# Second attention of a gated transformer block: the inversion of the sums on ACT moved between two fours of exponentials, the division moved on VectorE

## The chip, the cores and the metric

The kernel runs on one core of a Trainium2 chip. The metric is the device time of one execution in microseconds (us). The engines are TensorE (PE, with its weight loads as PEld), VectorE (DVE), ScalarE (ACT), GpSimd (POOL) and SyncE (SP). Each runs its own instructions in program order, and they wait for each other on semaphores.

## The reference

Four stages follow one another on x of 32 batches x 128 rows x 128 columns: an attention over a context, six layers of local attention with an MLP, a second attention over the same context, and a quantised matrix product. The change lies in the third. Cut to what matters there:

```python
x = x + tanh(g_xattn[1]) * L1_xattn(layernorm(x), ctx, ctx)       # the third stage
x = x + tanh(g_ffn[1]) * L1_ffn(layernorm(x))                      # the fourth

# L1_xattn, 16 heads of 8 columns, for each batch
scores = einsum('bhqd,bhkd->bhqk', Qh, Kh) / sqrt(8)
scores = scores - max(scores, axis=-1)
attn = softmax(scores, axis=-1)
attn = clip(attn, 1e-12, None)
attn = attn / sum(attn, axis=-1)          # the second division: the sums inverted on ACT
ctx = einsum('bhqk,bhkd->bhqd', attn, Vh)
return ctx @ Wo.T + bo
```

## The kernel before

The stages run one after another. The last two are one pipeline, written in `second_attention`: a loop over steps from -18 to 47, in which each engine issues a fixed list of calls, each for a batch that lies some steps ahead or behind. `@each(NB)` drops the calls whose batch does not exist, and `@opening` keeps one in four, those that begin a group of four batches (128 rows each, so 512 columns). So the work of four successive steps repeats. In this text a **0-step** is a step whose number is a multiple of four, and the 1-step, 2-step and 3-step follow it.

What a batch b goes through, by the functions' names:

- PE `scores(b, half)` (L1337) makes the scores of heads 0 to 7 and 8 to 15, each half into two banks of PSUM of its own. It waits until the exponentials of batch b-1 have read that half (`exped[half]`).
- DVE `row_maxima(b, half)` (L1589) takes the maxima of the half, one step early for half 0.
- ACT `exponentials(b, half)` (L1480) makes eight exponentials of 128x128, one a head, each with its sum. It signals `exped[half]` after the eighth.
- DVE `invert(b, half)` (L1596) inverts these first sums, and POOL `normalise(b, half)` (L1710) multiplies by them.
- PE `transpose_weights(b, t)` (L1347) turns four heads, t = 0 to 3, called t0 to t3 below: t0 and t1 one step later, t2 and t3 two steps later. DVE `clip_weights(b, t)` (L1604) clips each into `probsT`.
- PE `mix(b)` (L1361 and L1365), in step b+2, multiplies the clipped weights by v and by ones. The second product is the sum that the clipped weights are divided by. It waits for the clipped t3 (`clipped`).
- ACT `invert_sums(b)`, in step b+2, inverts that sum as exp(-ln): one ACTIVATE with Ln (L1489) and one with Exp (L1491), both 128x128. It waits for `mixed`, and signals `den_inverted`.
- DVE `divide_mix(b)` (L1613), in step b+2, multiplies the mixed values by it and signals `mix_made`.

Four banks of PSUM rotate among all other products of PE (`ROTATING`). `Banks.fill` makes PE wait until the last user of a bank has been read. A bank that `mix` filled is free when `divide_mix` has signalled. By the table of turns, the next user of the bank of a 3-step's mix is t3 in the 0-step that follows; of a 0-step's mix it is `transpose_x`, of a 1-step's `project_out`, of a 2-step's t3 in the 3-step. The bank that `project_k` fills in a 1-step goes to t3 of the 2-step. It is free when DVE and ACT `bias_k` (L1581, L1452) have made the keys.

What else occurs once in four steps and is named below: in a 0-step ACT `copy_x` (L1509); in a 1-step PE `transpose_x` (L1383) and `project_k` (L1309), ACT `copy_steps` (L1528) and `bias_k`, DVE `row_stats` (L1623, L1627) and `bias_k`; in a 2-step ACT `square` (L1435) and `place_v` (L1472), DVE `rescale` (L1669) and `row_amax` (L1636); in a 3-step ACT `bias_q` (L1461) and `root` (L1441, L1443), DVE `row_scale` (L1643) and `quantise` (L1653, L1656, L1660). The functions on rows belong to the fourth stage and begin some steps later than the attention.

The lists of PE's calls in a step, which the change leaves alone (each opening one stands in its own kind of step only):

```python
scores(step, 0); transpose_weights(step - 2, 2); project_out(step - 6); mean(step + 6)
transpose_weights(step - 2, 3); transpose_x(step - 9); scores(step, 1); multiply(step - 14)
transpose_weights(step - 1, 0); transpose_steps(step - 13); project_q(step + 1)
mix(step - 2); transpose_weights(step - 1, 1); project_k(step + 3); variance(step + 5); project_v(step + 2)
```

Of the kernel before, what the change touches and what calls it, by code (L numbers as in the profile page):

```python
# [64 lines left out]
def each(n):  # L65

    def of(stage):
        def run(u, *more):
            if 0 <= u < n:
                stage(u, *more)  # L70
        return run
    return of
# [46 lines left out]
def build(nc, dram):  # L119
    stack = ExitStack()  # L120
    with stack:
# [3 lines left out]
        def sem(name):  # L125
            return stack.enter_context(nc.semaphore(name))
# [1058 lines left out]
        def second_attention(phase):  # L1185
# [43 lines left out]
            scored, maxed, exped, normalised = ([sem(f"x1_{k}{half}") for half in range(2)] for k in ("scored", "maxed", "exped", "normalised"))  # L1229
# [33 lines left out]
            def bank(stage, n):  # L1263
                return psum[:, bank_of[stage, n], :]
# [159 lines left out]
            def act(act):  # L1424
# [4 lines left out]
                @each(NB)  # L1429
                @opening  # L1430
                def square(g):
                    act.wait_ge(ln_centred_made, before + g + 1)
                    if g >= 2:
                        act.wait_ge(ln_scaled, before + g - 1)
                    act.activation(spread[g % 2][:, :], centred[g % 2][:, :], ACT.Square).then_inc(ln_squared, 1)  # L1435
# [19 lines left out]
                @each(NB)  # L1455
                @opening
                def bias_q(g):
                    act.wait_ge(q_projected, g + 1)
                    if g >= 2:
                        act.wait_ge(scored[1], GB * (g - 1))  # L1460
                    act.activation(queries[g % 2][:, :], bank("q", g), ACT.Identity, bias=b_q, scale=inv_root).then_inc(biased_act, 1)  # L1461
# [10 lines left out]
                    act.copy(places[:, :, :, 0:XD], bank("v", g).rearrange("p (m j d) -> p j m d", j=4, d=XD)).then_inc(v_placed, 1)  # L1472

                @each(NB)
                def exponentials(b, half):
                    act.wait_ge(maxed[half], b + 1)
                    if b >= 2:
                        act.wait_ge(turned, TURNS * (b - 2) + 2 * half + 2)
                    for h in range(8 * half, 8 * half + 8):
                        e = act.activation(expo[b % 2][:, h, :], psum[:, 4 + h // 4, (h % 4) * S:(h % 4 + 1) * S], ACT.Exp,  # L1480
                                           bias=negmax[b % 2][:, h:h + 1], accum_out=total[b % 2][:, h:h + 1])
                    e.then_inc(exped[half], 1)

                @each(NB)
                def invert_sums(b):
                    act.wait_ge(mixed, b + 1)
                    if b >= 2:
                        act.wait_ge(mix_made, b - 1)
                    act.activation(rden[b % 2][:, :], bank("mix", b)[:, S:2 * S], ACT.Ln).then_inc(den_logged, 1)  # L1489
                    act.wait_ge(den_logged, b + 1)  # L1490
                    act.activation(rden[b % 2][:, :], rden[b % 2][:, :], ACT.Exp, scale=-1.0).then_inc(den_inverted, 1)  # L1491
# [30 lines left out]
                @each(NB)  # L1522
                @opening
                def copy_steps(g):
                    act.wait_ge(steps_turned, g + 1)
                    if g >= 2:
                        act.wait_ge(multiplied, g - 1)
                    act.copy(stepsT[g % 2][:, :], bank("tq", g)[:, 0:GT // 2].bitcast(BF16)).then_inc(steps_copied, 1)  # L1528

                for step in range(FIRST, LAST):  # L1530
                    exponentials(step, 0)
                    square(step + 6)
                    copy_steps(step - 13)
                    bias_q(step + 1)
                    invert_sums(step - 2)
                    exponentials(step, 1)
                    place_v(step + 2)
                    row_root(step - 9)
                    bias_k(step + 3, 2)
                    bias_k(step + 3, 3)  # L1540
                    root(step + 5)
                    copy_x(step - 8)
                    gate_out(step - 5)

            def dve(dve):
# [29 lines left out]
                @each(NB)  # L1575
                @opening
                def bias_k(g, j):
                    dve.wait_ge(k_projected, g + 1)
                    if g >= 2:
                        dve.wait_ge(scored[1], GB * (g - 1))  # L1580
                    dve.tensor_scalar(keys[g % 2][:, j, :], bank("k", g), head_parts[:, j:j + 1], b_k_part[:, j:j + 1],  # L1581
                                      ALU.mult, ALU.add).then_inc(biased_dve, 1)

                @each(NB)
                def row_maxima(b, half):
                    dve.wait_ge(scored[half], b + 1)
                    if b >= 2:
                        dve.wait_ge(exped[half], b - 1)
                    dve.tensor_reduce(negmax[b % 2][:, 8 * half:8 * half + 8], pairs[2 + half].rearrange("p (h n) -> p h n", h=8),  # L1589
                                      axis=X, op=ALU.max, negate=True).then_inc(maxed[half], 1)  # L1590

                @each(NB)
                def invert(b, half):
                    t8 = total[b % 2][:, 8 * half:8 * half + 8]
                    dve.wait_ge(exped[half], b + 1)
                    dve.reciprocal(t8, t8).then_inc(inverted, 1)  # L1596
# [10 lines left out]
                @each(NB)  # L1607
                def divide_mix(b):
                    g = b // GB
                    dve.wait_ge(den_inverted, b + 1)  # L1610
                    if g >= 2:
                        dve.wait_ge(out_made, g - 1)
                    dve.tensor_tensor(mixedT[g % 2][:, (b % GB) * S:(b % GB + 1) * S], bank("mix", b)[:, 0:S], rden[b % 2][:, :],  # L1613
                                      ALU.mult).then_inc(mix_made, 1)
# [57 lines left out]
                for step in range(FIRST, LAST):  # L1672
                    clip_weights(step - 2, 2)
                    centre(step + 6)
                    clip_weights(step - 2, 3)
                    row_scale(step - 11)
                    rescale(step - 14)
                    row_maxima(step, 1)
                    clip_weights(step - 1, 0)
                    if step > FIRST:  # L1680
                        residual(step - FIRST)
                    invert(step, 0)
                    row_amax(step - 10)
                    quantise(step - 11)
                    row_stats(step - 9)
                    divide_mix(step - 2)
                    clip_weights(step - 1, 1)
                    bias_k(step + 3, 0)
                    row_maxima(step + 1, 0)
                    invert(step, 1)  # L1690
                    bias_k(step + 3, 1)
# [208 lines left out]
```

## Time and profile before

| what | us |
|---|---|
| median of 3 runs | 3399.71 |
| lowest and highest | 3399.1, 3406.09 |
| the profiled execution, its own time | 3404.29 |
| its span, first to last instruction | 3402.5 |
| of that the last two stages, from about 3060 to the end | 342.5 |
| of that the steps 0 to 31 with their drain, from the first scores at 3096 | 306 |

The profiled execution took 1.8 us more than its span, and lies 4.6 us above the median of the runs. Busy times of the whole span (PE 95%, DVE 86%, ACT 70%, POOL 78%) are those of the six layers before; they say nothing of the last 340 us. A group of steps is read there from four views: the windows (busy time of each engine and the granted TensorE clock), the timeline of one engine with the idle time before each row, one line's instructions with what they wait for, and the chain of waits. All times in the rows are microseconds from the span's start.

### The profile page before, as it was taken

Reading aid. Unit: us, or ns where it says so; the run is one execution under the profiler, and the core shown is the slowest. Engines: PE = TensorE matmul, PEld = TensorE weight load, DVE = VectorE, ACT = ScalarE, POOL = GpSimd, SP = SyncE. Lnnn points to the kernel's source line nnn. Section 1 sums busy time; section 2 is a strip of 40 time slices with the busy share of each in tenths; the row PEclk is TensorE's granted clock in tenths of the full one; section 3 lists DMA queues with packets and bytes.
Section 4 is the critical chain, followed back from the end, with each engine's and each line's share of the span. In section 5 each row is a group of like instructions: output and inputs, shape, how many; then the busy total and the mean of one; then the engine's idle time right before and its main releaser. Section 6 shows DMA issues by size and latency. Waiting matters only on the chain. (4 is left out here: it accounts for less than half of the span.)

```text
span 3402.5 us, 130907 instructions
## 1 busy us (share of the span) xinstructions
PE 3247.4 (95%) x56355; PEld 2059.5 (61%) x56386; DVE 2942.0 (86%) x3343; ACT 2379.8 (70%) x4288; POOL 2640.0 (78%) x1408
## 2 busy tenths in 40 slices
PE   8977999999999999999999999999999999977996
PEld 4544666666666666666666666666666666643554
DVE  6869999999999999999989899998999999935887
ACT  6865676767676667777677776776767676746895
POOL 1218988888888888888888888888888888833576
PEclk9989999999999999999999999999999999988998
DMA  2001433333433343333433334343344333340000
GB/s 94 2 1 56 121 114 114 121 121 115 119 112 114 120 126 120 114 114 122 126 111 117 114 111 129 117 120 114 114 126 126 118 111 113 109 125 1 2 11 17
DMA packets 229189, 336.06 MB, mean 99 GB/s; under 512 B 39046, under 2 KB 151044, under 8 KB 228228
## 3 DMA queue, kind: packets, MB, share of 16 engines
q1 hardware_dynamic: 228612, 327.68, 31.5%
q8 instruction: 446, 7.31, 0.9%
q14 instruction: 131, 1.07, 0.1%
HBM read 124.14 MB, written 102.76 MB: 67 GB/s over the span
## 5 line engine op out<-in xcount | busy, mean ns | idle before, releaser
L733 PE MATMUL psum<-w_qkv,f_xs 128*128 128x512 f32 x2304 | 1078.3, 604 | 12.3 <-DVE f_times_sin L1027 7.6
L1154 POOL TENSOR_TENSOR f_rotated<-f_times_cos,f_times_sin 128x1024 f32<-128x1024 f32 x384 | 908.4, 2366 | 8.8 <-DVE f_times_sin L1027 8.8
L1162 POOL TENSOR_TENSOR f_rotated<-f_rotated,f_rnorm 128x1024 f32<-128x1024 f32 x384 | 723.0, 1903 | 31.8 <-ACT f_rnorm L908 4.9
L733 PEld LDWEIGHTS psum<-w_qkv,f_xs 128*128 128x128 f32 x2304 | 409.8, 191 | 395.1 <-issue 375.2
L897 ACT ACTIVATE f_squares<-psum 128x1024 f32<-128x1024 f32 x384 | 393.0, 1023 | 341.0 <-PE psum L733 335.9
L1146 POOL TENSOR_TENSOR f_probs<-f_probs,f_rowsum 128x1024 f32<-128x1024 f32 x192 | 365.4, 1903 | 322.3 <-DVE f_rowsum L1066 322.3
L1026 DVE TENSOR_TENSOR f_times_cos<-psum,rot 128x1024 f32<-128x1024 f32 x384 | 470.0, 1224 | 121.8 <-ACT f_squares L897 117.7
L915 ACT COPY f_qkT<-psum 128x1024 f32<-128x1024 f32 x384 | 369.9, 1013 | 210.2 <-PE psum L743 210.2
L1027 DVE TENSOR_TENSOR f_times_sin<-psum,rot 128x1024 f32<-128x1024 f32 x384 | 466.4, 1214 | 0.0
L1034 DVE TENSOR_REDUCE f_sumsq<-f_squares 128x16 f32<-128x1024 f32 x384 | 463.8, 1210 | 0.0
L743 PEld LDWEIGHTS psum<-consts,f_rotated 128*128 128x128 f32 x3072 | 348.6, 141 | 96.3 <-issue 87.6
L743 PE MATMUL psum<-consts,f_rotated 128*128 128x128 f32 x3072 | 371.2, 274 | 16.2 <-POOL f_rotated L1162 13.3
L1140 POOL TENSOR_TENSOR f_probs<-f_probs,f_negmax 128x1024 f32<-128x1024 f32 x192 | 365.0, 1901 | 0.0
L787 PEld LDWEIGHTS psum<-f_probsT,f_v 64*64 64x64 f32 x6144 | 262.7, 135 | 162.5 <-issue 162.5
L801 PE MATMUL psum<-f_outT,w_o 128*128 128x256 f32 x1536 | 358.9, 387 | 1.2 <-ACT f_outT L929 1.2
L760 PEld LDWEIGHTS psum<-f_qkT 64*32 64x32 f32 x24576 | 254.0, 105 | 146.9 <-issue 143.1
L787 PE MATMUL psum<-f_probsT,f_v 64*64 64x64 f32 (+1 forms) x6144 | 309.7, 228 | 15.6 <-issue 15.6
L801 PEld LDWEIGHTS psum<-f_outT,w_o 128*128 128x128 f32 x1536 | 285.8, 191 | 45.2 <-issue 1.8
L787 PE MATMUL psum<-f_probsT,f_v_moved 64*64 64x32 f32 (+1 forms) x12288 | 307.1, 217 | 0.0
L760 PE MATMUL psum<-f_qkT 64*32 64x64 f32 x24576 | 285.2, 226 | 1.3 <-issue 1.3
L787 PEld LDWEIGHTS psum<-f_probsT,f_v_moved 64*64 64x64 f32 x12288 | 285.8, 136 | 0.0
L828 PE MATMUL psum<-f_xn,w 128*128 128x512 f32 (+1 forms) x576 | 278.3, 607 | 7.4 <-ACT f_xn L971 7.4
(175 smaller groups left out, 5173.5 us busy)
## 6 DMA issues: line engine op xcount, KB each, us to landing
f_v_moved<-f_v SPq DMA_DIRECT2D x768, 128.0 KB, 2.8
turned_blocks<-w_qkv SPq DMA_DIRECT2D x192, 512.0 KB, 3.0
f_probsT<-turned_blocks SPq DMA_DIRECT2D x768, 128.0 KB, 2.8
w_qkv<-in_l_wqkv SPq DMA_DIRECT2D x18, 512.0 KB, 4.2
w_o<-in_l_wo SPq DMA_DIRECT2D x6, 512.0 KB, 4.5
w_qkv<-in_ctxT SPq DMA_DIRECT2D x1, 2048.0 KB, 8.7
out<-x_f_result SPq DMA_DIRECT2D x8, 256.0 KB, 2.2
w<-in_l_w SPq DMA_DIRECT2D x6, 341.0 KB
```

Source lines behind the costliest of these rows:

```text
L733: mm = pe.matmul(pairs[i][:, j * BANK:(j + 1) * BANK], xs[g % 2][:, u % GB, :], w_qkv[:, part * INNER + j * BANK:part * INNER + (j + 1) * ...
L743: tr = pe.transpose(pairs[i][:, t * S:(t + 1) * S], rotated[u % 2][:, part, 2 * t:2 * t + 2, :].rearrange("p h d -> p (h d)"), ident)
L760: mm = pe.matmul(pairs[i][these, at:at + NEAR], qkT[u % 2][rows, 0, t, these], qkT[u % 2][rows, 1, t, near], start=True, stop=True, tile_p ...
L787: mm = pe.matmul(pairs[i][cols, at + windows.start * WIN:at + windows.stop * WIN], values, probsT[u % 2][rows, windows, j, :], start=True, ...
L801: mm = pe.matmul(pairs[i][:, 0:GT // 2], w_o[:, t, :], outT[:, t, tokens], start=t == 0, stop=t == IT - 1)
L897: act.activation(squares[part][:, :], pair("qk"[part], u), ACT.Square).then_inc(squared[part], 1)
L915: act.copy(qkT[u % 2][:, part].rearrange("p t n -> p (t n)"), pair(("qT", "kT")[part], u)).then_inc(copied[part], 1)
L1026: dve.tensor_tensor(halves(times_cos[part][:, :]), halves(taken), table(0), ALU.mult)
L1027: dve.tensor_tensor(halves(times_sin[part][:, :]), halves(taken)[:, ::-1], table(1), ALU.mult).then_inc(producted[part], 1)
L1034: dve.tensor_reduce(sumsq[u % 2][:, part * H:(part + 1) * H], squares[part][:, :].rearrange("p (s h d) -> p h s d", s=2, h=H), axis=XY, op ...
L1154: pool.tensor_tensor(rotated[u % 2][:, part].rearrange("p h (s d) -> p s h d", s=2), halves(times_cos[part][:, :]), halves(times_sin[part] ...
L1162: pool.tensor_tensor(rt, rt, rnorm[u % 2][:, part * H:(part + 1) * H].unsqueeze(2).broadcast_to([P, H, HD]), ALU.mult).then_inc(normalised ...
```

## The change

ACT's exponentials of a half can now be issued in part, by the first and the last head. Half 0 is issued whole. Half 1 is issued as two fours, and the inversion of the sums, which stood ahead of half 1, now stands between them. `exped[1]` is signalled behind the second four, as before behind the eighth. On DVE the division moves two places back: behind `clip_weights(step - 1, 1)` and the first `bias_k`, ahead of `row_maxima(step + 1, 0)`. Nothing is added, removed or resized, and PE and POOL keep their order.

```diff
@@ -1472,14 +1472,15 @@
                 @each(NB)
-                def exponentials(b, half):
+                def exponentials(b, half, first, last):
                     act.wait_ge(maxed[half], b + 1)
                     if b >= 2:
                         act.wait_ge(turned, TURNS * (b - 2) + 2 * half + 2)
-                    for h in range(8 * half, 8 * half + 8):
+                    for h in range(8 * half + first, 8 * half + last):
                         e = act.activation(expo[b % 2][:, h, :], psum[:, 4 + h // 4, (h % 4) * S:(h % 4 + 1) * S], ACT.Exp,
                                            bias=negmax[b % 2][:, h:h + 1], accum_out=total[b % 2][:, h:h + 1])
-                    e.then_inc(exped[half], 1)
+                    if last == 8:
+                        e.then_inc(exped[half], 1)
@@ -1528,12 +1529,13 @@
                 for step in range(FIRST, LAST):
-                    exponentials(step, 0)
+                    exponentials(step, 0, 0, 8)
                     square(step + 6)
                     copy_steps(step - 13)
                     bias_q(step + 1)
+                    exponentials(step, 1, 0, 4)
                     invert_sums(step - 2)
-                    exponentials(step, 1)
+                    exponentials(step, 1, 4, 8)
                     place_v(step + 2)
@@ -1683,9 +1685,9 @@
                     row_stats(step - 9)
-                    divide_mix(step - 2)
                     clip_weights(step - 1, 1)
                     bias_k(step + 3, 0)
+                    divide_mix(step - 2)
                     row_maxima(step + 1, 0)
```

ACT in a 3-step and the beginning of the 0-step behind it, before (L1461 is `bias_q`, L1441 and L1443 `root`; the names behind waits are semaphores):

```order
L1461 ACTIVATE x_queries<-psum,x_vecs 128x512 [waits x1_scored1,x1_q_projected]
L1489 ACTIVATE x_rden<-psum 128x128 [waits x1_mix_made,x1_mixed]
L1491 ACTIVATE x_rden<-x_rden 128x128 [waits x1_den_logged]
L1480 ACTIVATE x_expo,x_total<-psum,x_negmax 128x128 [waits x1_turned,x1_maxed1]
L1480 ACTIVATE x_expo,x_total<-psum,x_negmax 128x128 x7
L1441 ACTIVATE x_spread<-psum,eps 128x512 [waits ln_variance_made]
L1443 ACTIVATE x_spread<-x_spread 128x512 [waits ln_logged]
```

The same place after:

```order
L1461 ACTIVATE x_queries<-psum,x_vecs 128x512 [waits x1_scored1,x1_q_projected]
L1480 ACTIVATE x_expo,x_total<-psum,x_negmax 128x128 [waits x1_turned,x1_maxed1]
L1480 ACTIVATE x_expo,x_total<-psum,x_negmax 128x128 x3
L1490 ACTIVATE x_rden<-psum 128x128 [waits x1_mix_made,x1_mixed]
L1492 ACTIVATE x_rden<-x_rden 128x128 [waits x1_den_logged]
L1480 ACTIVATE x_expo,x_total<-psum,x_negmax 128x128 [waits x1_turned,x1_maxed1]
L1480 ACTIVATE x_expo,x_total<-psum,x_negmax 128x128 x3
L1441 ACTIVATE x_spread<-psum,eps 128x512 [waits ln_variance_made]
L1443 ACTIVATE x_spread<-x_spread 128x512 [waits ln_logged]
```

Four exponentials moved ahead of the two ACTIVATEs of the inversion; it is the same in every other step, whatever stands around.

DVE from the end of `quantise` in a 3-step into the 0-step behind it, before:

```order
L1660 TENSOR_SCALAR x_f_steps<-x_f_cen 128x512 [waits f1_quantised]
L1613 TENSOR_TENSOR x_mixedT<-psum,x_rden 128x128 [waits x1_out_made,x1_den_inverted]
L1604 TENSOR_SCALAR x_probsT<-psum 128x512 [waits x1_mixed,x1_turned]
L1589 TENSOR_REDUCE x_negmax<-psum 128x8 [waits x1_exped0,x1_scored0]
L1596 RECIPROCAL x_total<-x_total 128x8 [waits x1_exped1]
L1604 TENSOR_SCALAR x_probsT<-psum 128x512 [waits x1_mixed,x1_turned] x2
```

The same place after (lines of DVE stand two higher in the changed file):

```order
L1662 TENSOR_SCALAR x_f_steps<-x_f_cen 128x512 [waits f1_quantised]
L1606 TENSOR_SCALAR x_probsT<-psum 128x512 [waits x1_mixed,x1_turned]
L1615 TENSOR_TENSOR x_mixedT<-psum,x_rden 128x128 [waits x1_out_made,x1_den_inverted]
L1591 TENSOR_REDUCE x_negmax<-psum 128x8 [waits x1_exped0,x1_scored0]
L1598 RECIPROCAL x_total<-x_total 128x8 [waits x1_exped1]
L1606 TENSOR_SCALAR x_probsT<-psum 128x512 [waits x1_mixed,x1_turned] x2
```

The division and the clip of t1 changed places.

DVE in a 1-step, from the end of `row_stats`, before:

```order
L1627 BN_AGGR x_f_meanvar<-x_f_stats 128x2 x3
L1613 TENSOR_TENSOR x_mixedT<-psum,x_rden 128x128 [waits x1_out_made,x1_den_inverted]
L1604 TENSOR_SCALAR x_probsT<-psum 128x512 [waits x1_mixed,x1_turned]
L1581 TENSOR_SCALAR x_keys<-psum,consts,x_bk_part 128x512 [waits x1_scored1,x1_k_projected]
L1589 TENSOR_REDUCE x_negmax<-psum 128x8 [waits x1_exped0,x1_scored0]
```

The same place after:

```order
L1629 BN_AGGR x_f_meanvar<-x_f_stats 128x2 x3
L1606 TENSOR_SCALAR x_probsT<-psum 128x512 [waits x1_mixed,x1_turned]
L1583 TENSOR_SCALAR x_keys<-psum,consts,x_bk_part 128x512 [waits x1_scored1,x1_k_projected]
L1615 TENSOR_TENSOR x_mixedT<-psum,x_rden 128x128 [waits x1_out_made,x1_den_inverted]
L1591 TENSOR_REDUCE x_negmax<-psum 128x8 [waits x1_exped0,x1_scored0]
```

Here the division also passed the first part of the keys.

## Rows read from the trace of the kernel before

**Rows 1.** Windows over four steps: us, busy (x) of PE PEld DVE ACT POOL, clock.

```profile
3273.80:3308.30 34.50, 31.45 (x384) 19.24 (x384) 29.65 (x58) 31.06 (x149) 24.18 (x17) 1.00 0.03 9
```

**Rows 2.** Line L1489, the Ln of the inversion: its instructions and their waits.

```profile
L1489 ACT ACTIVATE x_rden<-psum x32: 277/277/334, 3117.6 to 3375.5; 128x128 f32<-128x128 f32 x32
  PE psum L1365: 22.1, 27
```

**Rows 3.** ACT's waits from 3130 to 3330: us in total, times, longest.

```profile
ACT x_rden L1489 <- PE psum L1365: 12.1, 21, 2.0
```

**Rows 4.** Timeline of ACT, a 0-step: start, us, row, [idle before <-releaser].

```profile
3267.01 0.37 ACT L1480 ACTIVATE x_expo<-psum,x_negmax 128x128 f32<-128x128 f32 x1 [0.61 <-DVE x_negmax L1589]
...
3269.42 0.40 ACT L1480 ACTIVATE x_expo<-psum,x_negmax 128x128 f32<-128x128 f32 x1
...
3270.35 0.28 ACT L1489 ACTIVATE x_rden<-psum 128x128 f32<-128x128 f32 x1 [0.44 <-PE psum L1365]
...
3270.88 0.35 ACT L1480 ACTIVATE x_expo<-psum,x_negmax 128x128 f32<-128x128 f32 x1
```

**Rows 5.** Timeline of ACT, a 2-step in which the inversion did not wait.

```profile
3321.13 0.42 ACT L1480 ACTIVATE x_expo<-psum,x_negmax 128x128 f32<-128x128 f32 x1
3321.47 0.33 ACT L1489 ACTIVATE x_rden<-psum 128x128 f32<-128x128 f32 x1
...
3322.06 0.35 ACT L1480 ACTIVATE x_expo<-psum,x_negmax 128x128 f32<-128x128 f32 x1
```

**Rows 6.** Timeline of PE, the same 0-step (t3, t0, mix) into the 1-step.

```profile
3265.30 0.66 PE L1347 MATMUL psum<-consts,x_expo 128*128 128x128 f32 x4 [0.52 <-DVE x_mixedT L1613]
...
3266.95 0.66 PE L1347 MATMUL psum<-consts,x_expo 128*128 128x128 f32 x4
3268.34 1.08 PE L1361 MATMUL psum<-x_probsT,x_vpad 128*32 128x128 f32 x32 [0.74 <-issue]
...
3273.81 1.13 PE L1337 MATMUL psum<-x_keys,x_queries 32*128 32x512 f32 x4 [0.41 <-ACT x_expo L1480]
```

**Rows 7.** Timeline of DVE, from the 3-step through the 0-step.

```profile
3264.96 0.28 DVE L1613 TENSOR_TENSOR x_mixedT<-psum,x_rden 128x128 f32<-128x128 f32 x1
3265.16 0.68 DVE L1604 TENSOR_SCALAR x_probsT<-psum 128x512 f32<-128x512 f32 x1
3265.76 1.21 DVE L1589 TENSOR_REDUCE x_negmax<-psum 128x8 f32<-128x1024 f32 x1
...
3267.00 1.24 DVE L1604 TENSOR_SCALAR x_probsT<-psum 128x512 f32<-128x512 f32 x2
...
3271.00 0.29 DVE L1613 TENSOR_TENSOR x_mixedT<-psum,x_rden 128x128 f32<-128x128 f32 x1 [0.86 <-ACT x_rden L1491]
```

**Rows 8.** Timeline of DVE, `row_maxima` of half 0 in a 1-step.

```profile
3245.72 1.23 DVE L1589 TENSOR_REDUCE x_negmax<-psum 128x8 f32<-128x1024 f32 x1 [0.23 <-PE psum L1337]
```

**Rows 9.** Timelines of ACT and PE in the first groups, before `quantise` has begun.

```profile
3125.66 0.28 ACT L1489 ACTIVATE x_rden<-psum 128x128 f32<-128x128 f32 x1 [0.72 <-PE psum L1365]
...
3136.44 1.13 PE L1337 MATMUL psum<-x_keys,x_queries 32*128 32x512 f32 x4 [1.06 <-ACT x_expo L1480]
...
3169.22 1.13 PE L1337 MATMUL psum<-x_keys,x_queries 32*128 32x512 f32 x4 [0.62 <-ACT x_expo L1480]
```

**Rows 10.** Chain of waits, from the 1-step into the 2-step: start, us, what.

```profile
3247.98 1.39 issue
```

**Rows 11.** The drain: ACT in a 1-step, and PE's t3 after the last batch's scores.

```profile
3345.24 0.28 ACT L1489 ACTIVATE x_rden<-psum 128x128 f32<-128x128 f32 x1 [0.19 <-PE psum L1365]
...
3364.61 0.66 PE L1347 MATMUL psum<-consts,x_expo 128*128 128x128 f32 x4 [3.02 <-DVE x_mixedT L1613]
```

**Rows 12.** The clock: PE's window (us, busy, clock), ACT in that 2-step, ACT in a later one.

```profile
3180.70:3183.90 3.20, 3.20 (x52) 0.55 0.02 5
...
3184.86 0.28 ACT L1489 ACTIVATE x_rden<-psum 128x128 f32<-128x128 f32 x1 [1.97 <-PE psum L1365]
...
3253.77 0.28 ACT L1489 ACTIVATE x_rden<-psum 128x128 f32<-128x128 f32 x1 [0.53 <-PE psum L1365]
```

## The prediction, made before the changed kernel was run

> **What bounds the kernel now.** The change touches only the last two stages, some 300 of 3400 us, so I read those. First the windows over four steps: in their middle they repeat to 0.1 us, 34.5 us each (three groups, of which one row stands for all), with PE busy 31.4, ACT 31.1 and DVE 29.6 of them at a clock of 1.00 [rows 1]. No engine is full, and three are nearly so; the time is then set by a loop of waits that passes through all three, and a wait that goes is worth only what the next one allows.
>
> Next the line of the inversion: 27 of its 32 Ln wait for the mix's second product, 22.1 us in all [rows 2], 12.1 of them in the 200 us between 3130 and 3330 [rows 3]. That is what the change can remove. Last the timelines and the chain, to see in which steps that wait lies on the loop. I follow a group from scores of half 1 in a 1-step to the same place four steps later:
>
> - From the 1-step to the 2-step the loop runs through PE's scores, the maxima on DVE, the keys on DVE and then on ACT. PE's t3 of the 2-step wants the bank of `project_k` and stands 1.39 us, which the chain calls issue [rows 10], since it names no releaser; by the table of banks it is ACT's keys. ACT's own speed does not matter in this piece, as it waits for DVE's keys itself.
> - From there to the 3-step PE runs without a gap, and from its scores for the 3-step DVE runs without one through `quantise` and into the 0-step. ACT's waits of the 2-step (0.53 [rows 12]) and of the 3-step (0.73, the same pattern) are not on the loop: at its end ACT stands 0.61 us for DVE's maxima in any case [rows 4].
> - In the 0-step DVE clips t2 and t3 until 3268.24 [rows 7], the mix starts at 3268.34 [rows 6], and ACT, done with half 0, stands 0.44 us for the mix before it can invert [rows 4]. Then come the eight exponentials of half 1, and PE stands 0.41 us for them [rows 6]. This wait is on the loop, once in four steps.
>
> **The change part by part.**
>
> *The wait of a 0-step.* With an exponential last started at 3269.42 and the next free place 0.34 later, ACT would begin half 1 at 3269.76. It began at 3270.88 [rows 4], 1.12 later, of which an inversion that waits for nothing takes 0.59 (3321.47 to 3322.06 [rows 5]). So 0.53 us is removed from ACT there: the mix ends at 3270.3, four exponentials at 0.34 end at 3271.1, and the inversion then finds its sum ready. The eighth exponential ends 0.53 earlier. PE can use only 0.41 of it, since that is how long it stood [rows 6]; then its own work, which began with the mix, is last. **0.41 us a group.** It holds for the five groups between 3169 and 3341, which have the same gap of 0.41: 5 x 0.41 = 2.05 us.
>
> *The two groups before them* have no `quantise`, DVE is not last, and ACT's wait in the 3-step (0.72 [rows 9]) counts: ACT gains 0.72 + 0.06 = 0.78, and PE stood 1.06 at the end of the first and 0.62 at the end of the second [rows 9]. The first gives 0.78, the second 0.62: 1.40 us. In the steps ahead of them the inversion waited for nothing, or not yet ran: nothing.
>
> *The drain.* In the last group no keys are made, so that the waits of the 0-step and the 1-step (0.53, and 0.19 + 0.06 [rows 11]) add up on ACT, and POOL's normalisation hands on 0.78 where PE took 0.41 of it: 0.37 us more.
>
> *The division moved on DVE.* It now stands behind one clip, 0.60 from start to start [rows 7], and in a 1-step also behind the first keys. Where DVE was waiting for ACT it fills the wait: in the 0-step DVE stood 0.86 us [rows 7], and the clip of t1 fits in. The inverted sum now comes at about 3271.7 in place of 3270.97, the division ends near 3272.0, just when `row_maxima` can start. In the 3-step DVE has no gap, the sum of its work is the same, and only the order changes: `row_maxima` starts as before, and the division is 0.60 later. PE's t3 of the 0-step waits for just that: 0.52 us before [rows 6], about 1.1 now. Behind t3 are queued the scores of half 1, t0 and the mix. They would be done 0.60 later, but the mix waits for the clipped t3 anyway, and that gap is 0.74 [rows 6]. So 0.14 us of cover is left, and I cost it at nothing. Without the cover each of six groups would lose up to 0.19: 0.60 less the 0.41 that PE has to spare. In the 1-step `row_maxima` stood 0.23 for PE's scores [rows 8]; the keys now start when `project_k` ends and the division (0.21 from start to start) ends 0.1 us ahead of the scores. Nothing, with little to spare. In the drain t3 is waited for with no cover: the clip of t3 comes 0.15 later than it would. I take 0.15 off.
>
> *The split itself.* One more instruction with waits a step, which are met. Where one half follows another with its wait, the start comes 0.34 to 0.36 behind the last, so at most 0.02 x 32 = 0.6 us of ACT, on the loop in a quarter of the steps: 0 to 0.2, taken as 0.1.
>
> **The sum:** 2.05 + 1.40 + 0.37 - 0.15 - 0.1 = 3.6 us less. The profiled execution would go from 3404.3 to 3400.7, its span from 3402.5 to 3398.9. The median of the runs is 4.6 us below the profiled one; by it 3399.7 - 3.6 = **3396.1 us**. That is 0.11% less. About 0.2%, or 6.8 us, is what a measurement of this kernel can tell from no change, so I forecast a gain that is hardly seen.
>
> **Rivals.**
>
> *All of ACT's wait counts.* ACT is busy 31 of 34.5 us [rows 1], and if my loop is wrong and ACT sets it, every removed microsecond shows: 12.1 us in 200, over the 237 us from the first inversion to 3355, is 14.3 us, giving 3385.4. Half of it, 7 us, is the point from which it is a measurable gain. For it speaks that PE waits for ACT's exponentials in most 0-steps. Against it stand PE's gap of 0.41 as a cap, and the 0.61 us in which ACT waits for DVE with no regard to the inversion [rows 4, 6].
>
> *PE is last everywhere.* If PE's 0.41 is in truth covered (a weight load or the bank behind it), the exponentials gain nothing that PE can take, and only the first groups stay: 3398 to 3400, no change.
>
> *The later division starves PE, and its clock falls.* This is the one that ends slower. Its place is t3 of the 0-step, where PE's wait goes from 0.52 to 1.1 us. The clock did fall to the 1.2 GHz level once in these stages, to a mean of 0.55 from 3180.7 to 3183.9 [rows 12]; PE had just had the gap of 1.38 ahead of t3 in that 2-step. ACT then waited 1.97 for the mix where it waits 0.53 in the same place of later groups [rows 12], so a fall costs 1.44. If the longer wait brought one in each of the six groups from the first `quantise` on, and the cover of 0.14 failed too, the cost is 6 x (1.44 + 0.19) = 9.8 us: 3409.5. It decides from about two falls on, where 2 x 1.63 = 3.3 has eaten most of the gain. Against it: the other gaps of 1.39 us in later groups brought no fall, the clock of whole groups stays at 1.00 [rows 1], and PE's idle time as a whole shrinks by the 0.41.
>
> The Trainium skill ("TensorE: Matmul & The Clock Gate", section "HAM oscillation — how this bites in real kernels") says that PE's short idles between groups of matmuls can make the clock go up and down, and this speaks against lengthening a wait of PE. By it the time would be that of this rival, 3409.5; by the rows, in which such gaps recur without a fall, it is that of the sum. I go by the rows.
>
> **How the numbers follow.** My forecast, 3391 to 3400: 0.62. PE last everywhere, 3398 to 3401: 0.17. ACT's wait counting half or whole, 3385 to 3393: 0.14. Starved PE, 3401 to 3410: 0.07. Faster by over 0.2% (below 3392.9) comes from the third and an edge of the first: 0.16. Slower by over 0.2% (above 3406.5) is half of the last and a bit of spread, as one of three runs lay at 3406.09: 0.05. Within 0.2%: 0.79. The range from 3390 to 3401.5 leaves out the lower part of the third and most of the last.
>
> **What would show it.** Right: the line of Ln has almost no idle time before it outside the drain; the period goes from 34.5 to about 34.05 us; PE's gap ahead of scores of half 1 in 1-steps is gone, and its gap ahead of t3 in 0-steps is about 1.1 us; ACT's wait for the maxima in 0-steps and for the keys in 1-steps is larger than before (0.61 for the maxima), since ACT arrives earlier at both. Wrong: a period below 33.8 (then ACT was last in more steps than one); a period of 34.4 or more, with the mix of the 0-step starting later after the clip of t3 than 0.1 us, or DVE's maxima in the 1-step behind the division and not behind the scores; or a clock under 1.00 in more than one group. A single fall of the clock that comes or goes moves the result by 1.4 us and would say nothing of the change.

## The result, and the profile after

| kernel | median of 8 runs, us | lowest and highest |
|---|---|---|
| before | 3404.2 | 3397.32, 3408.96 |
| changed | 3416.41 | 3410.62, 3420.55 |

The ratio is 1.0029, 95% interval 1.0015 to 1.0043. So the changed kernel is slower by 0.3%, about 10 us (5 to 15), where the prediction said 3.6 us faster. The time lies above its range. Some 4.5 us of the distance to the predicted 3396.1 are not the change's: the median of the kernel before is 3404.2 with eight runs, where the prediction had three runs and 3399.71. A second round of runs later gave 1.0013 (0.9998 to 1.0028), on the same side, but by itself not told from no change.

The stages ahead of the second attention vary by some microseconds from one execution to the next: the first scores of half 0 began at 3096.32 in the profile before and at 3103.10 in the one after. What the change does is read better from there to the end of the span. I call it **the stage** below: 3402.5 - 3096.3 = 306.2 us before, 3418.2 - 3103.1 = 315.1 us after. It grew by 8.9 us.

The windows over four steps of the changed kernel (us, busy (x) of PE PEld DVE ACT POOL, then the granted clock as a share of 2.4 GHz), for [rows 1]:

```profile
3214.50:3249.80 35.30, 32.77 (x385) 20.39 (x384) 29.60 (x58) 31.16 (x148) 24.17 (x17) 0.95 0.03 9
3249.80:3286.80 37.00, 34.47 (x385) 20.99 (x384) 29.69 (x58) 31.26 (x148) 24.19 (x18) 0.91 0.03 9
```

A group of steps takes 35.3 to 37.0 us in place of 34.5. DVE's and ACT's busy times are as before (29.6 and 31.1 to 31.3). PE is busy for 1.4 to 3.1 us more with the same instructions, and the clock is below 1.00. The timeline of PE in the 0-step of the second window, for [rows 6] (start, us, row, idle before):

```profile
3276.31 0.79 PE L1347 MATMUL psum<-consts,x_expo 128*128 128x128 f32 x4 [1.15 <-DVE x_mixedT L1615]
3277.04 2.07 PE L1337 MATMUL psum<-x_keys,x_queries 32*128 32x512 f32 x4
3279.04 1.11 PE L1347 MATMUL psum<-consts,x_expo 128*128 128x128 f32 x4
3280.09 1.94 PE L1361 MATMUL psum<-x_probsT,x_vpad 128*32 128x128 f32 x32
3281.80 1.90 PE L1365 MATMUL psum<-x_probsT,x_ones 128*32 128x128 f32 x32
```

t3 waits 1.15 us for the division, where it waited 0.52. Behind it scores take 2.07 in place of 1.13 and the mix 1.94 in place of 1.08. The clock of these few microseconds is that of the lower level, 1.2 GHz:

```profile
3276.30:3283.60 7.30, 7.29 (x76) 0.53 0.12 36
3265.50:3276.30 10.80, 9.67 (x101) 1.00 0.01 2
```

(PE's window: us, busy, clock.) Ahead of the wait the clock was at 2.4 GHz. The Trainium skill ("TensorE: Matmul & The Clock Gate", section "A second HAM failure mode: psum-queue depth-cycling") tells of another kernel in which short idles of PE between groups of matmuls make the clock go up and down. In this profile the trace agrees: 0.53 of full speed behind a wait of 1.15 us.

ACT in the same 0-step, for [rows 4]:

```profile
3277.43 0.37 ACT L1480 ACTIVATE x_expo<-psum,x_negmax 128x128 f32<-128x128 f32 x1 [1.36 <-DVE x_negmax L1591]
...
3283.77 0.28 ACT L1490 ACTIVATE x_rden<-psum 128x128 f32<-128x128 f32 x1 [1.84 <-PE psum L1365]
```

Four exponentials now stand ahead of the inversion, and still it waits 1.84, because the mix is late by more than they take. Over the line as a whole (us, times) the wait has shrunk from 22.1 [rows 2] to:

```profile
  PE psum L1365: 14.5, 9
```

of which 6.17 and 1.49 are in the drain. DVE did what its new order says, for [rows 7]:

```profile
3240.05 0.68 DVE L1606 TENSOR_SCALAR x_probsT<-psum 128x512 f32<-128x512 f32 x1
3240.65 0.28 DVE L1615 TENSOR_TENSOR x_mixedT<-psum,x_rden 128x128 f32<-128x128 f32 x1
3240.85 1.22 DVE L1591 TENSOR_REDUCE x_negmax<-psum 128x8 f32<-128x1024 f32 x1
```

### The profile page after: what moved, and what is told of

Same layout as the page of the kernel before. It is cut to its first block and busy times, and to the rows that moved or that the text cites. A ratio compares the mean times of both kernels' runs of the same rounds, so it can differ in the third digit from the quotient of the medians.

```text
span 3418.2 us, 130937 instructions
## 1 busy us (share of the span) xinstructions
PE 3264.5 (96%) x56355; PEld 2067.2 (60%) x56386; DVE 2942.0 (86%) x3343; ACT 2381.3 (70%) x4288; POOL 2640.0 (77%) x1408
```

## The experiments

I count a **fall** where the first product of a mix takes 1.5 us or more in place of 1.08. (One row of `after_again` has only 4 of its 32 records; there the second product starts 1.70 us after the first, as behind the other falls.) Other falls lie in the 2-steps 6 and 10 and in the drain; they make the stage longer, and the count of four leaves them out. Four 0-steps of each profile count for the wait of t3: those of the steps 12, 16, 20 and 24, from the first `quantise` to the drain. `dve_long`, `fill_half`, `fill_one`, `shift_once` and `dve_again` were run once each, for the profile, and have no ratio. "Period" is from one such group to the next, by the transposes of x.

| kernel | edit | ratio (95%) | stage, us | t3's wait in 0-steps | falls in those four | period without, with fall |
|---|---|---|---|---|---|---|
| before | | | 306.2 | 0.52 | 0 | 34.46 |
| changed | both | 1.0029 (1.0015-1.0043) | 315.1 | 1.15 | 4 | -, 35.3 to 37.0 |
| after_again | both | 1.0013 (0.9998-1.0028) | 315.0 | 1.15 | 4 | -, 35.3 to 37.0 |
| act_only | split only | 1.0016 (1.0005-1.0027) | 311.6 | 0.55 | 0 | 35.03 |
| dve_only | later division only | 0.9993 (0.9984-1.0002) | 305.0 | 1.10 | 0 | 34.46 |
| dve_again | the same | | 304.9 | 1.10 | 0 | 34.46 |
| late_in_3 | division later in 3-steps only | 0.9992 (0.9982-1.0002) | 310.0 | 1.11 | 1 | 34.46, 37.44 |
| back_in_3 | both, division back in 3-steps | 0.9982 (0.9971-0.9992) | 301.9 | 0.55 | 0 | 33.98 |
| back_again | the same | 0.9982 (0.9969-0.9995) | 304.7 | 0.55 | 0 | 33.98 |
| fill_gap | both, 4 transposes in the wait | 0.9992 (0.9978-1.0005) | 301.2 | 0.71 | 0 | 33.98 |
| fill_half | both, 2 transposes | | 305.0 | 0.93 | 0 | 33.98 |
| fill_one | both, 1 transpose | | 304.9 | 1.04 | 0 | 33.98 |
| pad_in_1 | both, 4 transposes in 1-steps | 1.0011 (0.9997-1.0025) | 313.8 | 1.15 | 3 | 34.41, 35.8 to 37.4 |
| shift_once | both, 12 transposes once | | 301.3 | 1.15 | 0 | 33.97 |
| dve_long | division only, later still | | 320.7 | 2.24 | 3 | 35.39, 37.0 to 39.9 |
| turns | back_in_3 and other banks | 0.9992 (0.9981-1.0003) | 302.5 | 0.31 | 0 | 33.13 |
| turns2 | the same, in all steps | 0.9977 (0.9964-0.9991) | 299.5 | 0.31 | 0 | 33.13 |

The theory after the result was the rival of the prediction: the later division makes PE wait longer ahead of t3, and its clock falls. Against it stood that the split of the exponentials costs the time, or that the falls are chance.

### Each half of the change alone

`act_only` has the split with the division at its old place:

```diff
+                    exponentials(step, 1, 0, 4)
                     invert_sums(step - 2)
-                    exponentials(step, 1)
+                    exponentials(step, 1, 4, 8)
```

> The exponentials of half 1 in two fours with the inversion between them, as in the changed kernel; the division on DVE stays where it was before. If the later division makes the loss (PE's t3 of a 0-step waits 1.15 us and the clock falls behind it): that wait is 0.5 us again, the granted clock of the groups from the first quantise on is 1.00, their period 34.1 to 34.5 us, the ratio to before 0.999 to 1.000. If the split of the exponentials makes the loss: periods of 35 to 37 us and a ratio of 1.002 to 1.003, as in the changed kernel. If falls of the clock are chance: some groups with one and some without, in this as in the others.

t3's wait in the 0-step was short and there was no fall behind it, as the first expectation had it, but the period of 35.03 and the ratio of 1.0016 lie near what was expected if the split made the loss. The reason is another wait. DVE in a 1-step:

```profile
3213.80 0.29 DVE L1615 TENSOR_TENSOR x_mixedT<-psum,x_rden 128x128 f32<-128x128 f32 x1 [1.04 <-ACT x_rden L1492]
3214.01 0.68 DVE L1606 TENSOR_SCALAR x_probsT<-psum 128x512 f32<-128x512 f32 x1
3214.60 0.80 DVE L1583 TENSOR_SCALAR x_keys<-psum,consts,x_bk_part 128x512 f32<-128x512 f32 x1
```

The inverted sum comes later, by the four exponentials, and DVE stands 1.04 us for it with the clip, the keys and the maxima queued behind. The keys then reach ACT late, and PE's t3 of the 2-step waits 2.40 in place of 1.39. The period is 35.03. In one such 2-step the clock fell too:

```profile
3253.99 0.63 PE L1347 MATMUL psum<-consts,x_expo 128*128 128x128 f32 x4 [2.40 <-issue]
...
3256.86 1.94 PE L1361 MATMUL psum<-x_probsT,x_vpad 128*32 128x128 f32 x32
```

DVE stands so long in each 1-step from the first `quantise` to the drain. So the split needs the division moved in the 1-steps. It is the 3-steps in which the move hurts.

`dve_only` is the reverse, and `late_in_3` the smallest edit that lengthens the wait:

```diff
+                    if step % 4 != 3:
                         divide_mix(step - 2)
                     clip_weights(step - 1, 1)
                     bias_k(step + 3, 0)
+                    if step % 4 == 3:
+                        divide_mix(step - 2)
```

> The division on DVE stands later as in the changed kernel; ACT's order stays as before. Later division: t3 of a 0-step waits 1.1 us, clock of a group 0.91 to 0.95, period 36 to 37 us, ratio 1.002 to 1.004 (ACT's wait for the mix stays, so up to 0.001 worse than the changed kernel). Split: as before, period 34.5, ratio 1.000.

> The kernel before, but in the 3-steps alone the division stands behind the clip of t1. It is the smallest edit that lengthens PE's wait. Later division: t3 of a 0-step waits 1.1 us, the clock falls in most groups, ratio 1.002 to 1.004. Any other cause: 1.000.

Both missed. The wait was 1.10, as said, but the time did not change: in `dve_only` the clock fell in none of the four 0-steps, in `late_in_3` in one. Here are two waits of `late_in_3`, one with a fall and one without:

```profile
3226.68 0.66 PE L1347 MATMUL psum<-consts,x_expo 128*128 128x128 f32 x4 [1.12 <-DVE x_mixedT L1613]
...
3230.19 1.94 PE L1361 MATMUL psum<-x_probsT,x_vpad 128*32 128x128 f32 x32
```

```profile
3263.90 0.66 PE L1347 MATMUL psum<-consts,x_expo 128*128 128x128 f32 x4 [1.11 <-DVE x_mixedT L1613]
...
3266.34 1.08 PE L1361 MATMUL psum<-x_probsT,x_vpad 128*32 128x128 f32 x32
```

It also shows that the later division costs nothing when the clock holds: the period of `dve_only` is 34.46, as before. The cover of 0.14 us ahead of the mix was there.

### The division back in the 3-steps

`back_in_3` keeps both halves of the change and takes the division back where DVE has no gap:

```diff
+                    if step % 4 == 3:
+                        divide_mix(step - 2)
                     clip_weights(step - 1, 1)
                     bias_k(step + 3, 0)
+                    if step % 4 != 3:
                         divide_mix(step - 2)
```

> The changed kernel, but in the 3-steps alone the division stands before the clip of t1 again. Later division: t3 of a 0-step waits 0.5 us, no fall of the clock from the first quantise on, period 34.0 to 34.1, ratio 0.9985 to 0.9995, which is the gain of the sum (3.6 us). If any of the other edits costs the time, the ratio stays at 1.002 to 1.003.

> The changed kernel with the division back in the 3-steps, once more, beside the next one on the same chip. The stage from the first scores to the end was 301.4 us in its first profile against 306.2 before. Again no fall of the clock between the first quantise and the drain, period 33.98, stage 301 to 303, ratio 0.997 to 0.999.

The ratio was 0.9982 twice. The period is 33.98 with no fall in eight 0-steps of two profiles:

```profile
3253.64 0.66 PE L1347 MATMUL psum<-consts,x_expo 128*128 128x128 f32 x4 [0.55 <-DVE x_mixedT L1615]
...
3256.67 1.08 PE L1361 MATMUL psum<-x_probsT,x_vpad 128*32 128x128 f32 x32 [0.74 <-issue]
...
3261.13 0.60 PE L1383 MATMUL psum<-consts,xres 128*128 128x128 f32 x4
```

The stage took 301.9 us in the first profile and 304.7 in the second; the second had two falls in earlier 2-steps, at 3152 and 3186, the first none.

### Something in the wait

`fill_gap` leaves the wait's end where it is and lets PE make the transposes of t2 twice in the 0-steps, ahead of it. Only work is added:

```diff
-                    for r in range(4):
-                        tr = pe.transpose(...)
+                    for _ in range(2 if t == 2 and b % 4 == 2 else 1):
+                        for r in range(4):
+                            tr = pe.transpose(...)
```

> The changed kernel, but in the 0-steps PE makes the four transposes of t2 twice (same operands, same bank), which puts 0.5 to 0.6 us of its work into the wait ahead of t3 and takes nothing off what it waits for. If the idle time in that place brings the fall: wait 0.6 us, no falls there, period 34.0, ratio 0.998 to 0.999, faster by 3 to 12 us with four transposes a group more. If the later division itself costs the time, or transposes are as good as idleness: falls as before, ratio 1.002 to 1.004.

```profile
3223.64 0.66 PE L1348 MATMUL psum<-consts,x_expo 128*128 128x128 f32 x4 [0.71 <-DVE x_mixedT L1616]
3224.22 1.13 PE L1337 MATMUL psum<-x_keys,x_queries 32*128 32x512 f32 x4
...
3226.08 1.08 PE L1362 MATMUL psum<-x_probsT,x_vpad 128*32 128x128 f32 x32
```

With four transposes more in each of those steps no fall came in four, the period was 33.98 and the stage 301.2 us, 14 less than the changed kernel's. Not all of the 14 are the transposes' doing: this profile also lacks the two falls in the steps 6 and 10 that both profiles of the changed kernel have. The ratio, 0.9992, has an interval that reaches to 1, but it lies below the 1.0013 of the changed kernel on the same chip; the medians of 12 runs each are 3403.48 and 3410.54. The later division stayed, and its cost went. The time is lost by the fall, not by what the division makes late.

The granted clock of all runs, not of the profiled ones alone, says the same. Over the whole span its mean is 0.9796 in the 12 runs of the changed kernel, 0.9818 in the 12 of `fill_gap` and 0.9817 in the 35 of the kernel before beside them. As an estimate, 0.0022 less over 3407 us is 15 us more at half clock; where PE is last, half of that is lost, 7.5 us. The medians of the first two differ by 7.1.

Two and one of the four transposes shorten the wait less:

> As fill_gap, but only two of the four transposes of t2 are made twice: t3's wait is 0.9 us, between the 0.71 that brought no fall in four places and the 1.15 that brought four of four in two profiles. If it is a matter of how long PE stands there, falls in some or none of the groups: the period is 34.0 without, 35.3 to 37 with.

> The changed kernel, and one of the four transposes of t2 is made twice in the 0-steps: t3's wait is about 1.04 us, between 0.93 (no fall in four) and 1.15 (eight of eight). If the length alone decides, and 1.10 brought one in twelve: none or one of four, period 33.98. If the split with its period makes the difference: falls in most.

Neither had a fall in a 0-step. Together: none in 12 with waits of 0.71 to 1.04 us. Both had falls in two earlier 2-steps, behind waits of 1.38 and 1.45, which is why their stages are longer than that of `fill_gap`. The changed kernel had those two as well, so the fair comparison is with them: 304.9 and 305.0 us against 315.1. In `fill_one`, step 6 and then step 16:

```profile
3149.14 0.63 PE L1348 MATMUL psum<-consts,x_expo 128*128 128x128 f32 x4 [1.39 <-issue]
...
3151.87 1.94 PE L1362 MATMUL psum<-x_probsT,x_vpad 128*32 128x128 f32 x32
...
3234.86 0.33 PE L1348 MATMUL psum<-consts,x_expo 128*128 128x128 f32 x1 [1.04 <-DVE x_mixedT L1616]
...
3237.30 1.08 PE L1362 MATMUL psum<-x_probsT,x_vpad 128*32 128x128 f32 x32
```

### Length, or place in time

> The changed kernel once more, for a second profile beside the others. If the falls of the clock belong to this kernel: again a fall behind t3's wait of 1.15 us in the 0-steps, four of four, and a ratio near 1.003. If they depend on where in time the wait happens to lie: some other number of falls, from 1 to 4.

> The changed kernel, but in the 1-steps from 9 on PE makes the transposes of x twice, 0.5 us, so that it does not get ahead of ACT's exponentials and a group without a fall takes 34.5 us as before, in place of 34.0; t3's wait of 1.15 us in the 0-steps stays. If the wait together with the split brings the fall in every group: four falls, period 35.5 to 37.5, ratio 1.003 to 1.005. If a fall depends on how the waits lie in time, which the period sets (the late division alone, at 34.46 us a group, had a fall in none and in one of four groups): at most one or two falls, ratio 1.000 to 1.002, faster than the changed kernel with more work in it.

> The later division alone, one more profile. In its first, t3 waited 1.10 us in four 0-steps and the clock fell in none. If the wait alone decides, as I had written ahead of the first, it must fall now. If the wait and where it lies in time decide, a period of 34.46 without falls repeats: 0 or 1 of 4.

> The later division alone, ACT as before, and in the 3-steps the division goes behind row_maxima as well: t3 waits 2.2 us in place of 1.10. If the length of the wait decides: a fall of the clock in four of four 0-steps. If the split has to be there, or the period of 34 us: none or one. Without a fall the longer wait costs 1.1 us a group less what PE has to spare (0.41), so a period of 35.1; with falls 36.5 to 38.

> The changed kernel, and in step 13 alone PE makes the transposes of x four times, which delays everything behind it once by about 1 us. All 0-steps keep their wait of 1.15 us. If the length of the wait decides: falls in all four 0-steps, with the same intervals of 35.3 and 37.0 us. If the place in time decides: a fall is missing, or starts at another place in its group, in the 0-steps behind step 13.

The changed kernel's second profile was the first's twin: the same intervals to 0.02 us, four falls of four. `dve_again` repeated its own, none of four at 1.10. `pad_in_1` (the transposes of x twice in every 1-step) had three, and its fourth wait of 1.15 brought none; its ratio does not tell it from the changed kernel. `dve_long`, with the division behind `row_maxima` in the 3-steps, had three of four behind 2.24 us, and the wait of 2.25 between them none. Its longest period, 39.9, has a fall in the 2-step besides.

`shift_once` is the changed kernel with twelve transposes more in step 13 alone:

```diff
-                    for n in range(GB):
-                        tr = pe.transpose(...)
+                    for _ in range(4 if g == 1 else 1):
+                        for n in range(GB):
+                            tr = pe.transpose(...)
```

Its four waits were 1.14 to 1.15, and the clock fell in none:

```profile
3200.11 0.66 PE L1347 MATMUL psum<-consts,x_expo 128*128 128x128 f32 x4 [1.15 <-DVE x_mixedT L1616]
...
3202.54 1.08 PE L1361 MATMUL psum<-x_probsT,x_vpad 128*32 128x128 f32 x32
```

```profile
3242.30:3276.30 34.00, 31.33 (x385) 19.23 (x384) 29.64 (x58) 31.07 (x150) 24.18 (x17) 1.00 0.03 10
```

The row at 3200.11 is of step 12, ahead of the only edit. Up to there this kernel is the changed one, which fell at that place in both of its profiles; and it had none of the two falls in earlier 2-steps either. So the edit did not prevent the first of them, and this run does not show what a shift does. What it shows is that executions of one instruction stream differ: with the same wait, the clock falls in some and holds in others. The length alone does not decide. That the place in time does is my reading and was not shown. What the profiles do show is that falls keep company. With waits of 1.14 and 1.15 us the 0-steps fell eleven times in twelve in the three profiles that had already fallen in the steps 6 and 10, and never in the one that had not. The earlier falls are not enough either: `back_again`, `fill_half` and `fill_one` had them too, and none in twelve 0-steps behind 0.55 to 1.04 us. In `shift_once`, step 6 kept its clock behind the same wait:

```profile
3151.60 0.63 PE L1347 MATMUL psum<-consts,x_expo 128*128 128x128 f32 x4 [1.38 <-issue]
...
3153.80 1.08 PE L1361 MATMUL psum<-x_probsT,x_vpad 128*32 128x128 f32 x32
```

This also tells what the change is worth without falls. The period is 33.97, the same as with the division back. The stage of 301.3 us has the added transposes in it, which made one period 35.29, 1.3 more; without them it would be 300.0 (an estimate).

### Other banks

The experiments pointed at PE's waits as the risk, and the largest left is the one of 1.38 us in the 2-steps, for the bank of the keys. `turns` lets t3 take the bank that t2 has left, and the multiply that of the keys, on top of `back_in_3`; `turns2` does it in every 2-step. The edit of `turns2` (that of `turns` has `stage == "mu"` in place of the three):

```diff
-            ROTATING = (("t2", 2, 1), ("out", 6, GB), ("mean", -6, GB), ("t3", 2, 1), ("tx", 9, GB), ("mu", 14, GB), ("t0", 1, 1),
+            ROTATING = (("t2", 2, 1), ("out", 6, GB), ("mean", -6, GB), ("mu", 14, GB), ("t3", 2, 1), ("tx", 9, GB), ("t0", 1, 1),
...
+                    elif stage in ("out", "mean", "mu") and step % GB == 2 and 0 <= step < NB:
+                        turn += 1
```

> The changed kernel with the division back in the 3-steps, and the table of banks changed: in the 2-steps t3 takes the bank that t2 left, and the multiply of the fourth stage that of the keys, so that PE no longer waits for ACT's keys ahead of t3. If the loop runs through those keys as the prediction had it: the wait of 1.38 us shrinks to 0.3 to 0.5, the period from 33.98 to 33.0 to 33.4, the ratio 0.995 to 0.998. If PE's wait there only moves to the next clip or to ACT: period 33.9, ratio 0.998.

> As turns, and now every 2-step gives turns to project_out, mean and multiply whether they exist or not, so that t3 never takes the bank of the keys: in turns it still did in the steps 2 and 26, with waits of 2.25 and 2.24 us. Period 33.13 as in turns, those two waits near 0.4, so 3.7 us less than turns: stage 298 to 300 us from the first scores, against 302.5 for turns and 301.4 for the kernel with the division back; ratio 0.996 to 0.998. If shorter waits in the middle are paid in the drain, as they were in part in turns, the stage stays at 301 to 302.

The wait is 0.41 us now, for the clip of t2, and the period 33.13, in both; these rows are from `turns2`:

```profile
3241.47 0.66 PE L1349 MATMUL psum<-consts,x_expo 128*128 128x128 f32 x4 [0.41 <-DVE x_probsT L1608]
```

```profile
3225.10:3258.30 33.20, 31.48 (x384) 19.29 (x386) 29.65 (x58) 30.71 (x148) 24.13 (x17) 1.00 0.04 11
```

`turns` measured 0.9992, hardly a gain, with a stage of 302.5. In the steps 2 and 26 t3 still took the keys' bank, with waits of 2.25 and 2.24, and the clock fell behind both. `turns2` mended that. Those two waits went to 1.26 and 1.27 and not to 0.4, with a fall behind the second alone; the stage is 299.5, and the ratio 0.9977 (0.9964 to 0.9991). It is the fastest kernel here, 0.2% below before and some 0.4 to 0.5% below the changed one (by its two ratios), though its interval does not part it from `back_in_3`.

## Why the prediction was wrong

- **What bounds the kernel: right.** The loop through PE, DVE and ACT, one wait of the 0-step on it and the keys' wait of the 2-step on it. `turns` shortened the latter, and the period went down by 0.85.
- **The wait of a 0-step, 0.41 us a group: right, and a little more.** The periods are 33.97 to 33.98 in place of 34.46, so 0.48. From t3 of the 2-step to t3 of the 0-step, and on to the transposes of x, nothing changed (15.94 and 7.5 us in both). The scores behind the transposes of x start 0.53 us after them (3261.66 against 3261.13) where they started 1.01 after (3273.81 against 3272.80). The idle time of 0.41 was counted from the modelled end of pipelined transposes; from start to start it was 0.48.
- **The stage without falls: right, or a little more.** 3.6 less predicted. `shift_once` without its added transposes is 300.0, so 306.2 - 300.0 = 6.2, but before had one fall, at 3181, worth 1.4 (its interval is 35.87 against 34.46). That leaves 4.8. Of these 1.4 lie in the drain, where the fall of before lasts longer: its interval there is 32.10, and that of `dve_only`, with the same order on ACT, 30.75. So 3.4 to 4.8 us are the change's own.
- **The later division costs nothing: the step that failed.** As a matter of what waits for what it held. The wait of t3 was put at 1.1 and is 1.15, the cover of 0.14 was there, and `dve_only` has the period of before. I had looked only at the order of work there, and gave the fall of the clock nothing in the sum. The 0.63 us of longer wait came with a fall of the clock, which lengthens a group from 33.98 to 35.3 or to 37.0, by whether it begins at the mix or already at scores: 1.3 to 3.0 us, where I had priced one at 1.44 from a single row. Of the prediction's own signs of being wrong, a clock under 1.00 in more than one group is the one that came.
- **The rival was priced and given 0.07.** It said 6 x 1.63 = 9.8 us more; 8.9 were measured on the stage and about 10 by the ratio. The sum was right by luck: there were four falls in 0-steps, not six, worth 10.3 together (3.0, 1.35 and twice 3.0); the cover of 0.14 held, where the rival let it fail; and it left out the gain of the new order. From 300.0 to 315.1 the falls cost 15.1, of which 4.8 lie in the steps 6 and 10 and in the drain and are not the longer wait's doing; the gain and the fall that before had, 6.2, took off the rest. The Trainium skill's sentence on short idles ("TensorE: Matmul & The Clock Gate", section "A second HAM failure mode: psum-queue depth-cycling"; the prediction gave the heading ahead of it) was named with 3409.5, and I weighed it by one argument of my own: gaps of 1.39 us recur without a fall. Those gaps were of another place, the 2-step, and one of the two early ones had a fall behind it. Nor had the clock fallen only "once in these stages": it fell also in the drain, where the first product of a mix takes 1.93 at 3366.51 in the profile before. A fall that had been seen behind a wait of 1.38 should have weighed more against a step that makes a second wait of that kind in every group.
- **The split costs 0.1 us: not told apart.** It is within what the stages differ by.
- **What I did not see at all** is what `act_only` showed: why the division was moved. Left at its place it makes DVE stand 1.02 to 1.04 us in every 1-step of the middle groups. The prediction took the move as given and priced it only for the waits that it makes.

What stays open is why the clock falls behind some waits of 1.1 to 1.2 us and not others. By counts: waits of 0.55 to 1.04 us none in 24 (with the split); of 1.10 to 1.12 one in 12; of 1.14 and 1.15 eleven in 16, but none of four in one execution; of 2.24 three in four. Length is a poor guide across places: the waits of 1.38 and 1.39 ahead of t3 in the 2-steps 14, 18 and 22, with other work of PE around them, brought one fall in 42 (fourteen profiles).

## What to carry to other kernels

A queue that is moved later by half a microsecond can be free by every wait in the trace and still cost three, if PE is what stands for it. Where a wait of PE passes about a microsecond in a loop, look for a fall of the granted clock behind waits of that length, above all at the place that changes, take its price from the lengthened group, and give it a chance that fits. The same edit in other steps, in which the moved work falls into an idle time that exists, is worth having: moving the division in three kinds of step out of four made a loss of 0.1 to 0.3% into a gain of 0.2%.

## What the runs showed of the hardware

- A fall lasts beyond the wait that precedes it: 7.3 us at a mean clock of 0.53 behind 1.15 us. Scores took 2.07 us in place of 1.13, a product of the mix 1.94 in place of 1.08.
- PE work added ahead of a wait can shorten the whole: one or two transposes a group made the stage 10 us shorter, 304.9 and 305.0 against 315.1, with the same two earlier falls in each.
- Up to step 12 the changed kernel and `shift_once` are the same instructions with the same waits; the clock fell in the steps 6, 10 and 12 in two executions and in none of them in the third. Runs of one kernel spread, and along their mean granted clock: the changed kernel's lay between 3398.48 us at 0.983 and 3422.93 at 0.975 in one set of 12. (The stages ahead have a share in that: the 35 runs of the kernel before beside them lay between 3395.86 at 0.985 and 3417.57 at 0.978.)
